# ScalarE applies the heads' norms in the launch block, and the low weight parts are dealt two and two to VectorE and GpSimd

## The chip, the cores and the metric

The kernel runs on one core of a Trainium2 chip. The metric is the time of one execution on the device in microseconds, lower is better. A core has TensorE (matrix products and turns into PSUM), VectorE, ScalarE and GpSimd (element by element work; the profile calls them PE, DVE, ACT and POOL), and SyncE, which issues DMAs here. Each engine works through its own queue in the order written; between engines, and where an engine reads what it has just written, semaphores order the work.

## The reference

The model has two layers, each of a cross attention, a self attention and a feed-forward part, on 256 tokens of width 512. All that this case touches are the projections at the head of the first one:

```python
def _ln(x, w, b):
    mu = jnp.mean(x, axis=-1, keepdims=True)
    var = jnp.mean(jnp.square(x - mu), axis=-1, keepdims=True)
    return (x - mu) * jax.lax.rsqrt(var + EPS) * w + b

def _fp8_linear_pertensor(x, wq, w_scale, in_scale):
    xq = _div_clamp_fp8(x, in_scale)
    return jnp.einsum('bsi,oi->bso', xq * in_scale, wq) * w_scale
...
ln_out = _ln(hidden_states, ln_w, ln_b)
q = _fp8_linear_pertensor(ln_out, wq, wq_scale, q_in_scale).reshape(b, s, g, hpg, d)
q = _ln(q, qln_w, qln_b)
k = _fp8_linear_pertensor(ln_out, wk, wk_scale, k_in_scale).reshape(b, s, g, d)
k = _ln(k, kln_w, kln_b)
v = _fp8_linear_pertensor(ln_out, wv, wv_scale, v_in_scale).reshape(b, s, g, d)
core = _gqa(q, k, v).reshape(b, s, nh * d)
qx = _fp8_linear_pertensor(ln_out, wqx, wqx_scale, qx_in_scale).reshape(b, s, g, hpg, d)
qx = _ln(qx, qxln_w, qxln_b)
```

Each head (128 columns) of q, qx and k gets a norm of its own over its columns; v gets none.

## The kernel before

The launch block is `front_stage`, the first stage with products. It cuts the four projections into twelve blocks of four heads (512 columns): four of q, four of qx, two of k, two of v. Each block is two steps, one for each half of the 256 tokens: steps 0 to 19 are those with a norm, 20 to 23 those of v. In the profile the names of this stage begin with `front_`.

**Weights.** A block's weights arrive in `raw` (three buffers, SyncE) as four slabs of 128x512. They are multiplied by the input scale and split into a rounded high part and the rest, the low part, so that a product of two passes keeps the precision. ScalarE makes the four high slabs (`high`, L2763). The low slabs are dealt by `POOL_KC` and `DVE_KC`: in a block with a norm VectorE makes slab 0 (`low`, one scalar_tensor_tensor, L2823) and GpSimd slabs 1 to 3, each with two operations (scale L2695, subtract L2702); in the blocks of v VectorE makes three and GpSimd one. High and low lie in a ring of four (`split`). A load into `raw` waits until high and both low halves of the block three before are done.

**A step.** TensorE makes the product of the step in eight 128x512 passes (`project`, L2732) into one of four PSUM tiles `mmp`. VectorE takes each head's mean and variance (`measure`: four bn_stats L2839, four bn_aggr L2842), ScalarE the root (`root`, L2779), VectorE the reciprocal (L2847) and then the norm itself, (product - mean) x rstd, one tensor_scalar for each of four heads (`normalise`, L2851) into `norm`, two buffers. TensorE turns the four heads (`turn`, L2742), and ScalarE puts them away with weight and bias (`put`, L2784). VectorE runs measure(s) ahead of normalise(s-1); TensorE runs project(s+3) right behind turn(s). Step s of VectorE also holds low(3 + s/2) for even s up to 16, and steps 4 and 8 a `quantise` (L2830 and L105 to L108), which makes the left operand for the next projection. ScalarE makes high(4 + s//2) in odd steps up to 15. In the first 40 us VectorE normalises x twice, and makes low(0) to low(3) and two quantises between.

All orders are written out by hand in each engine's loop. `measure(s)` waits for the count `norm` of step s-2, since `mv` and `stats` have two buffers; `link` makes an engine wait for its own operation.

## Time and profile before

| what | value |
|---|---|
| median of 3 runs | 2563.33 us (2561.70 to 2565.37) |
| the profiled execution | 2560.87 us |
| its span | 2559.1 us |
| mean granted TensorE clock | 0.959 |
| busy over the span: TensorE, VectorE, ScalarE, GpSimd | 89%, 70%, 47%, 23% |
| launch block, start to its last operation | about 4.9 to 130.4 us |

The profile comes from one execution. A group is a set of like instructions with its count, busy time and mean; a timeline row gives a start, a duration from the first start to the last end of the instructions merged in it, and what ended an idle stretch ahead of it. A waits row names who waited for whom. Of the span 5% is the launch block, and the stages behind it are left alone by the change.

### The profile page before, as it was taken

Reading aid. Unit: us, or ns where it says so; the run is one execution under the profiler, and the core shown is the slowest. Engines: PE = TensorE matmul, PEld = TensorE weight load, DVE = VectorE, ACT = ScalarE, POOL = GpSimd, SP = SyncE. Lnnn points to the kernel's source line nnn. Section 1 sums busy time; section 2 is a strip of 40 time slices with the busy share of each in tenths; the row PEclk is TensorE's granted clock in tenths of the full one; section 3 lists DMA queues with packets and bytes.
Section 4 is the critical chain, followed back from the end, with each engine's and each line's share of the span. In section 5 each row is a group of like instructions: output and inputs, shape, how many; then the busy total and the mean of one; then the engine's idle time right before and its main releaser. Section 6 shows DMA issues by size and latency. Waiting matters only on the chain. (4 is left out here: it accounts for less than half of the span.)

```text
span 2559.1 us, 31520 instructions
## 1 busy us (share of the span) xinstructions
PE 2279.3 (89%) x11472; PEld 1554.3 (61%) x11472; DVE 1786.6 (70%) x3422; ACT 1193.7 (47%) x1924; POOL 587.4 (23%) x435
## 2 busy tenths in 40 slices
PE   3779999999999999896897989788888779899998
PEld 2556666666666666564674456555556337677876
DVE  7856887777777778876896976666767754554444
ACT  4443466666566666633332114576766853211111
POOL 7810033334233333440000003323141300000000
PEclk9889999999999999998997999999999989899999
DMA  3331100000000100003544100000000013656661
GB/s 132 116 140 46 46 25 29 9 29 9 29 25 13 29 13 17 0 1 132 193 169 188 52 21 10 1 10 1 6 5 1 21 75 144 216 206 220 230 237 66
DMA packets 47622, 186.40 MB, mean 73 GB/s; under 512 B 6064, under 2 KB 10928, under 8 KB 37232
## 3 DMA queue, kind: packets, MB, share of 16 engines
q1 hardware_dynamic: 47472, 184.43, 20.0%
q8 instruction: 91, 1.49, 0.2%
q14 instruction: 59, 0.48, 0.1%
HBM read 174.71 MB, written 9.70 MB: 72 GB/s over the span
## 5 line engine op out<-in xcount | busy, mean ns | idle before, releaser
L406 PE MATMUL wide_a<-wide_w,ctxT 128*128 128x256 f32 (+1 forms) x2048 | 437.8, 367 | 2.8 <-POOL wide_eps L375 2.8
L406 PEld LDWEIGHTS wide_a<-wide_w,ctxT 128*128 128x128 f32 x2048 | 368.5, 191 | 76.5 <-issue 35.7
L388 POOL TENSOR_TENSOR wide_sums<-wide_sums,wide_s 128x512 f32<-128x512 f32 x224 | 301.3, 1345 | 461.8 <-ACT wide_s L536 448.6
L431 PE MATMUL wide_scores<-wide_q,wide_keysT 128*128 128x512 f32 x512 | 238.4, 604 | 12.5 <-ACT wide_s L532 12.5
L441 PE MATMUL wide_o<-wide_s,wide_values 128*128 128x512 f32 x512 | 233.8, 600 | 3.5 <-ACT wide_s L536 3.5
L532 ACT COPY wide_s<-wide_scores 128x512 f32<-128x512 f32 x256 | 148.4, 585 | 175.7 <-PE wide_scores L431 173.9
L1812 DVE TENSOR_REDUCE int_peaks<-int_a 128x1 f32<-128x1024 f32 x128 | 156.1, 1222 | 91.3 <-PE int_a L1535 90.1
L1535 PE MATMUL int_a<-int_keys,int_qrows 96*128 96x512 bf16 x512 | 151.8, 394 | 55.9 <-DVE int_peaks L1812 27.9
L1687 ACT ACTIVATE int_prob<-int_a,int_shift,int_qscale 128x1024 uint8<-128x1024 f32 x128 | 155.4, 1216 | 50.6 <-PE int_a L1535 50.1
L431 PEld LDWEIGHTS wide_scores<-wide_q,wide_keysT 128*128 128x128 f32 x512 | 87.9, 189 | 148.8 <-ACT wide_s L532 87.8
L594 DVE TENSOR_TENSOR wide_top<-wide_top,wide_s 128x512 f32<-128x512 f32 x240 | 165.6, 690 | 16.1 <-ACT wide_s L532 10.4
L2268 PEld LDWEIGHTS moe_bank<-moe_xb,moe_gate_up 128*128 128x128 f32 (+1 forms) x1536 | 162.0, 183 | 8.3 <-issue 8.3
L2268 PE MATMUL moe_bank<-moe_xb,moe_gate_up 128*128 128x96 f32 (+1 forms) x1536 | 162.6, 266 | 4.3 <-issue 4.3
L441 PEld LDWEIGHTS wide_o<-wide_s,wide_values 128*128 128x128 f32 x512 | 96.7, 192 | 100.2 <-issue 93.9
L607 DVE TENSOR_TENSOR wide_s<-wide_s,wide_peak_rows 128x2048 f32<-128x2048 f32 x64 | 146.8, 2294 | 0.8
L570 DVE BATCH_NORM_STATS2 wide_stats<-wide_keys 128x6 f32<-128x128 f32 x256 | 60.6, 278 | 110.9 <-ACT wide_values L514 108.4
L1446 PE MATMUL int_vp<-int_wk,ctxT_again 128*128 128x128 f32 x1024 | 126.6, 279 | 5.2 <-PEq L79 2.2
L1446 PEld LDWEIGHTS int_vp<-int_wk,ctxT_again 128*128 128x128 f32 x1024 | 122.7, 194 | 12.3 <-issue 4.0
L512 ACT COPY wide_keys<-wide_a 128x256 f32<-128x256 f32 x128 | 46.6, 364 | 174.3 <-PE wide_a L406 174.2
L536 ACT ACTIVATE wide_s<-wide_s 128x2048 f32<-128x2048 f32 x64 | 122.4, 1912 | 5.5 <-DVE wide_s L607 4.8
L1535 PEld LDWEIGHTS int_a<-int_keys,int_qrows 96*128 96x128 bf16 x512 | 37.0, 99 | 118.8 <-DVE int_peaks L1812 49.7
L2469 DVE TENSOR_REDUCE moe_coef<-moe_misc 96x1 f32<-96x4 f32 x32 | 5.1, 158 | 137.3 <-PE moe_misc L2277 137.3
(425 smaller groups left out, 4285.7 us busy)
## 6 DMA issues: line engine op xcount, KB each, us to landing
moe_gate_up<-hbm_m_gu SPq DMA_DIRECT2D x34, 1408.0 KB, 6.2
moe_down<-hbm_m_down_a SPq DMA_DIRECT2D x34, 512.0 KB, 6.9
causal_wqkv<-hbm_wqkv SPq DMA_DIRECT2D x8, 1536.0 KB, 6.6
ctxT<-hbm_ctxT SPq DMA_DIRECT2D x4, 2048.0 KB, 15.1
oproj_raw<-hbm_wproj SPq DMA_DIRECT2D x8, 1024.0 KB, 5.0
ctxT_again<-hbm_ctxT SPq DMA_DIRECT2D x4, 2048.0 KB, 21.6
wide_unit<-hbm_ffn_units SPq DMA_DIRECT2D x27, 256.0 KB, 2.7
ffn_early<-wide_unit SPq DMA_DIRECT2D x27, 256.0 KB, 2.0
```

What stands on the lines that cost most here:

```text
L388: ins = pool.tensor_tensor(sums[0][:, :], before, part[:, j, :], ALU.add)
L406: mm = pe.matmul(a[h][:, j, cols], ctxT[:, kc, t * P:(t + 1) * P], w[g % 2][:, kc, cols], start=(kc == 0), stop=(kc == KC - 1))
L431: pe.matmul(sp_[j % 2][:, :], keysT[:, j, :], q[:, :], start=True, stop=True).then_inc(s_s, 1)
L441: mm = pe.matmul(o[g % 2][:, :], values[m % VR][:, j, :], s[m % SR][:, j, :], start=(c == 0 and j == 0), stop=(c == QPG - 1 and j == 3))
L532: act.copy(s[n % SR][:, j, :], sp_[j % 2][:, :]).then_inc(s_se, 1)
L594: link(dve.tensor_tensor(top[:, :], before, s[n % SR][:, j, :], ALU.max))
L607: dve.tensor_tensor(s[m % SR][:, :, :], s[m % SR][:, :, :], peak_rows[:, :].unsqueeze(1).to_broadcast([P, 4, COLS]), ALU.subtract).then_in ...
L1446: mm = pe.matmul(vp[:, t * P:(t + 1) * P], ctxT[:, kc, i * P:(i + 1) * P], wk[:, kc, :], start=(kc == 0), stop=(kc == KC - 1))
L1535: mm = pe.matmul(wide[n % 2][:, z * 512:(z + 1) * 512], qrows[0:3 * HD, h, t * P:(t + 1) * P], keys[0:3 * HD, h % HC, j * 512:(j + 1) * 51 ...
L1687: act.activation(prob[u % 4][:, p * 1024:(p + 1) * 1024], wide[n % 2][:, :], ACT.Exp, bias=shift[:, u % NU:u % NU + 1], scale=qscale[:, t, ...
L1812: dve.tensor_reduce(peaks[u % 2][:, p:p + 1], wide[n % 2][:, :], AX.X, ALU.max).then_inc(s_ad, 1)
L2268: mm = pe.matmul(dst[0:m, j, :], wgu[i][:, kc, z * EI + f0:z * EI + f0 + m], xb[q % 2][:, kc, e % BATCH, :], start=(kc == 0), stop=(kc == ...
```

## The change

1. The deal of low slabs in the ten blocks with a norm becomes two and two: VectorE 0 and 1, GpSimd 2 and 3. The blocks of v stay.
2. VectorE no longer writes the norm. It makes the reciprocal and `centre` = -mean x rstd, a 128x4 operation, and counts `rstd` (`scale_of`). ScalarE's new `normalise` computes Identity(rstd x product + centre), one activation for each of four heads.
3. ScalarE runs root(s), then normalise(s-1), then put(s-2), then a high part. measure(s) keeps its wait for the norm of step s-2, which now is ScalarE's.

```diff
--- before.py
+++ after.py
@@ -2609,8 +2609,8 @@
                                               (3, "wv", 2, None, v)) for i in range(n)]
         NBK = len(blocks)
         NLN = 2 * sum(b[2] is not None for b in blocks)
-        POOL_KC = [range(1, KC) if b[2] is not None else range(3, KC) for b in blocks]
-        DVE_KC = [range(0, 1) if b[2] is not None else range(0, 3) for b in blocks]
+        POOL_KC = [range(2, KC) if b[2] is not None else range(3, KC) for b in blocks]
+        DVE_KC = [range(0, 2) if b[2] is not None else range(0, 3) for b in blocks]
         raw = [st.sb(f"raw{i}", [P, KC, HC * D]) for i in range(NRAW)]
         ring = [st.sb(f"split{i}", [P, 2, KC, HC * D], F32R) for i in range(NSPLIT)]
         scaled = [st.sb(f"scaled{i}", [P, HC * D]) for i in range(2)]
@@ -2631,15 +2631,16 @@
         mv = [st.sb(f"mv{i}", [P, HC, 2]) for i in range(2)]
         std = [st.sb(f"std{i}", [P, HC]) for i in range(2)]
         rstd = [st.sb(f"rstd{i}", [P, HC]) for i in range(2)]
+        centre = [st.sb(f"centre{i}", [P, HC]) for i in range(2)]
         norm = [st.sb(f"norm{i}", [P, HC, D]) for i in range(2)]
         mmp = [st.ps(f"mmp{i}", [P, HC, D]) for i in range(NMM)]
         tp = [st.ps(f"tp{i}", [P, HC, D]) for i in range(4)]
         s_x, s_scale, s_vec = st.sem("x_loaded"), st.sem("in_scales_loaded"), st.sem("vectors_loaded")
         s_raw = [st.sem(f"raw_loaded{i}") for i in range(NRAW)]
         names = ("identity var0 std0 norm0 turned0 lnT inverse divided quantised high low_dve low_pool eps "
-                 "products var std norm turned put stored dve pool")
+                 "products var std rstd norm turned put stored dve pool")
         (s_id, s_var0, s_std0, s_norm0, s_tp0, s_lnT, s_inv, s_y, s_q, s_hi, s_lod, s_lop, s_eps,
-         s_mm, s_var, s_std, s_norm, s_tp, s_put, s_st, s_dve, s_pool) = (st.sem(n) for n in names.split())
+         s_mm, s_var, s_std, s_rstd, s_norm, s_tp, s_put, s_st, s_dve, s_pool) = (st.sem(n) for n in names.split())
 
         def split(b):
             return ring[b % NSPLIT][:, 0, :, :], ring[b % NSPLIT][:, 1, :, :]
@@ -2775,8 +2776,17 @@
                     k = blocks[s // 2][0]
                     act.wait_ge(s_var, s + 1)
                     if s >= 2:
-                        act.wait_ge(s_norm, s - 1)
+                        act.wait_ge(s_rstd, s - 1)
                     act.activation(std[s % 2][:, :], mv[s % 2][:, :, 1], ACT.Sqrt, bias=eps_of[:, k:k + 1]).then_inc(s_std, 1)
+
+                def normalise(s):
+                    act.wait_ge(s_rstd, s + 1)
+                    if s >= 2:
+                        act.wait_ge(s_tp, s - 1)
+                    for h in range(HC):
+                        ins = act.activation(norm[s % 2][:, h, :], mmp[s % NMM][:, h, :], ACT.Identity, bias=centre[s % 2][:, h:h + 1],
+                                             scale=rstd[s % 2][:, h:h + 1])
+                    ins.then_inc(s_norm, 1)
 
                 def put(s):
                     _, _, ln, dst, i = blocks[s // 2]
@@ -2799,10 +2809,13 @@
                 act.wait_ge(s_eps, 1)
                 for s in range(NLN):
                     root(s)
+                    if s >= 1:
+                        normalise(s - 1)
                     if s >= 2:
                         put(s - 2)
                     if s % 2 and NSPLIT + s // 2 < NBK:
                         high(NSPLIT + s // 2)
+                normalise(NLN - 1)
                 for s in range(NLN, 2 * NBK):
                     k, _, _, dst, i = blocks[s // 2]
                     if s - 2 < NLN:
@@ -2842,15 +2855,13 @@
                         ins = dve.bn_aggr(mv[s % 2][:, h, :], stats[s % 2][:, h, :])
                     ins.then_inc(s_var, 1)
 
-                def normalise(s):
+                def scale_of(s):
                     dve.wait_ge(s_std, s + 1)
+                    if s >= 2:
+                        dve.wait_ge(s_norm, s - 1)
                     link(dve.reciprocal(rstd[s % 2][:, :], std[s % 2][:, :]))
-                    if s >= 2:
-                        dve.wait_ge(s_tp, s - 1)
-                    for h in range(HC):
-                        ins = dve.tensor_scalar(norm[s % 2][:, h, :], mmp[s % NMM][:, h, :], mv[s % 2][:, h, 0:1],
-                                                rstd[s % 2][:, h:h + 1], ALU.subtract, ALU.mult)
-                    ins.then_inc(s_norm, 1)
+                    dve.scalar_tensor_tensor(out=centre[s % 2][:, :], in0=mv[s % 2][:, :, 0], scalar=-1.0, in1=rstd[s % 2][:, :],
+                                             op0=ALU.mult, op1=ALU.mult).then_inc(s_rstd, 1)
 
                 dve.wait_ge(s_x, 16)
                 for r in range(2):
@@ -2887,12 +2898,12 @@
                 measure(0)
                 for s in range(1, NLN):
                     measure(s)
-                    normalise(s - 1)
+                    scale_of(s - 1)
                     if s in (4, 8):
                         quantise(s // 4 + 1)
                     if s % 2 == 0 and 3 + s // 2 < NBK:
                         low(3 + s // 2)
-                normalise(NLN - 1)
+                scale_of(NLN - 1)
                 dve.reciprocal(inv_smooth[:, :], smooth[:, :])
                 dve.tensor_tensor(wscale[:, :], scales[:, 4:5], scales[:, 5:6], ALU.mult)
```

VectorE's queue in the program of before, step 2 and the start of step 3 (`front_norm` is the count of norms done, `front_turned` that of turns):

```order
L2839 BN_STATS front_stats<-front_mmp 128x6 [waits front_norm,front_products]
L2839 BN_STATS front_stats<-front_mmp 128x6 x3
L2842 BN_AGGR front_mv<-front_stats 128x2 [waits front_dve]
L2842 BN_AGGR front_mv<-front_stats 128x2 x3
L2847 RECIPROCAL front_rstd<-front_std 128x4 [waits front_std]
L2851 TENSOR_SCALAR front_norm<-front_mmp,front_mv,front_rstd 128x128 [waits front_dve]
L2851 TENSOR_SCALAR front_norm<-front_mmp,front_mv,front_rstd 128x128 x3
L2823 SCALAR_TENSOR_TENSOR front_split<-front_raw,in_scales,front_split 128x512 [waits front_high]
L2839 BN_STATS front_stats<-front_mmp 128x6 [waits front_norm,front_products]
```

The same place of the changed program:

```order
L2852 BN_STATS front_stats<-front_mmp 128x6 [waits front_norm,front_products]
L2852 BN_STATS front_stats<-front_mmp 128x6 x3
L2855 BN_AGGR front_mv<-front_stats 128x2 [waits front_dve]
L2855 BN_AGGR front_mv<-front_stats 128x2 x3
L2862 RECIPROCAL front_rstd<-front_std 128x4 [waits front_std]
L2863 SCALAR_TENSOR_TENSOR front_centre<-front_mv,front_rstd 128x4 [waits front_dve]
L2836 SCALAR_TENSOR_TENSOR front_split<-front_raw,in_scales,front_split 128x512 [waits front_high]
L2836 SCALAR_TENSOR_TENSOR front_split<-front_raw,in_scales,front_split 128x512
L2852 BN_STATS front_stats<-front_mmp 128x6 [waits front_norm,front_products]
```

The four norms are gone from between a reciprocal and the next bn_stats, and the bn_stats still waits for `front_norm`, now a count of ScalarE's; the low operations are two.

ScalarE's queue before, steps 2 and 3 (`front_std` is the root, `qT` what put writes, `front_split` with 128x512 a high part):

```order
L2779 ACTIVATE front_std<-front_mv,front_eps_of 128x4 [waits front_norm,front_var]
L2784 ACTIVATE qT<-front_tp,head_vecs 128x4x128 [waits front_turned]
L2779 ACTIVATE front_std<-front_mv,front_eps_of 128x4 [waits front_norm,front_var]
L2784 ACTIVATE qT<-front_tp,head_vecs 128x4x128 [waits front_turned]
L2763 ACTIVATE front_split<-front_raw,in_scales 128x512 [waits front_products,front_raw_loaded2]
L2763 ACTIVATE front_split<-front_raw,in_scales 128x512 x3
```

And of the changed program:

```order
L2780 ACTIVATE front_std<-front_mv,front_eps_of 128x4 [waits front_rstd,front_var]
L2787 ACTIVATE front_norm<-front_mmp,front_centre,front_rstd 128x128 [waits front_rstd]
L2787 ACTIVATE front_norm<-front_mmp,front_centre,front_rstd 128x128 x3
L2794 ACTIVATE qT<-front_tp,head_vecs 128x4x128 [waits front_turned]
L2780 ACTIVATE front_std<-front_mv,front_eps_of 128x4 [waits front_rstd,front_var]
L2787 ACTIVATE front_norm<-front_mmp,front_centre,front_rstd 128x128 [waits front_turned,front_rstd]
L2787 ACTIVATE front_norm<-front_mmp,front_centre,front_rstd 128x128 x3
L2794 ACTIVATE qT<-front_tp,head_vecs 128x4x128 [waits front_turned]
L2764 ACTIVATE front_split<-front_raw,in_scales 128x512 [waits front_products,front_raw_loaded2]
```

Four activations on `front_norm` came in between root and put, waiting for `front_rstd`; the high part stands behind them and ahead of the next root.

## Rows read from the trace of the kernel before

**Rows 1.** Busy time by stretch: start:end, length, then engines, granted clock, DMA.
```profile
core 0: us, PE busy (x) PEld busy (x) DVE busy (x) ACT busy (x) POOL busy (x), PEclk, DMA share, GB/s
16.00:40.00 24.00, 9.73 (x32) 7.49 (x32) 21.04 (x25) 14.18 (x30) 23.22 (x14) 1.00 0.32 109
40.00:125.00 85.00, 56.27 (x227) 43.09 (x228) 78.52 (x285) 37.99 (x72) 74.70 (x50) 0.80 0.32 112
```

**Rows 2.** Groups up to 125 us: count, busy us, mean ns, idle before.
```profile
L2695 POOL TENSOR_SCALAR front_scaled<-front_raw,in_scales 128x512 f32<-128x512 f32 x32 | 57.4, 1793 | 7.8 <-DMA front_raw<-hbm_wq 7.8
...
L2702 POOL TENSOR_TENSOR front_split<-front_scaled,front_split 128x512 fp32r<-128x512 f32 x32 | 42.8, 1337 | 3.6 <-ACT front_split L2763 1.0
...
L2851 DVE TENSOR_SCALAR front_norm<-front_mmp,front_mv,front_rstd 128x128 f32<-128x128 f32 x80 | 27.3, 404 | 0.7
...
L108 DVE TENSOR_TENSOR front_quantised<-front_shifted,front_power 128x1024 fp32r<-128x1024 f32 x4 | 8.2, 2046 | 0.1
```

**Rows 3.** Waits up to 125 us: total us, times, longest.
```profile
ACT front_std L2779 <- DVE front_mv L2842: 51.0, 12, 9.1
...
PE front_tp L2742 <- DVE front_norm L2851: 29.2, 11, 8.0
```

**Rows 4.** Timeline of VectorE, step 5 and into 7: start, duration, operation, idle.
```profile
61.94 0.88 DVE L2839 BATCH_NORM_STATS2 front_stats<-front_mmp 128x6 f32<-128x128 f32 x4
...
63.15 0.14 DVE L2847 RECIPROCAL front_rstd<-front_std 128x4 f32<-128x4 f32 x1
63.33 1.37 DVE L2851 TENSOR_SCALAR front_norm<-front_mmp,front_mv,front_rstd 128x128 f32<-128x128 f32 x4
64.80 0.89 DVE L2839 BATCH_NORM_STATS2 front_stats<-front_mmp 128x6 f32<-128x128 f32 x4
...
69.32 0.89 DVE L2839 BATCH_NORM_STATS2 front_stats<-front_mmp 128x6 f32<-128x128 f32 x4 [1.09 <-PE front_mmp L2732]
```

**Rows 5.** Timeline of ScalarE in the same stretch.
```profile
63.47 0.76 ACT L2784 ACTIVATE qT<-front_tp,head_vecs 128x512 f32<-128x512 f32 x1
64.14 2.55 ACT L2763 ACTIVATE front_split<-front_raw,in_scales 128x512 fp32r<-128x512 f32 x4
66.58 0.29 ACT L2779 ACTIVATE front_std<-front_mv,front_eps_of 128x4 f32<-128x4 f32 x1
```

**Rows 6.** Groups of ScalarE over the whole span, shapes apart.
```profile
L2763 ACT ACTIVATE front_split<-front_raw,in_scales 128x512 fp32r<-128x512 f32 x48 | 30.6, 710 | 1.8 <-DMA front_raw<-hbm_wq 1.8
...
L946 ACT ACTIVATE causal_masked<-causal_masked,causal_inv 128x128 f32<-128x128 f32 x16 | 6.3, 393 | 7.2 <-DVE causal_inv L996 7.2
L2784 ACT ACTIVATE qT<-front_tp,head_vecs 128x512 f32<-128x512 f32 x8 | 6.1, 762 | 0.0
...
L2811 ACT ACTIVATE v<-front_mmp,scales 128x512 f32<-128x512 f32 x4 | 2.7, 683 | 1.6 <-PE front_mmp L2732 1.6
```

**Rows 7.** The line of VectorE's low slabs: count, shortest/median/longest ns, starts.
```profile
L2823 DVE SCALAR_TENSOR_TENSOR front_split<-front_raw,in_scales,front_split x16: 736/950/1783, 16.2 to 112.2; 128x512 fp32r<-128x512 f32 x16
```

**Rows 8.** Timeline of VectorE: first quantise, first bn_stats of a product, last quantise.
```profile
25.02 0.43 DVE L2830 TENSOR_SCALAR front_y<-front_y 128x1024 bf16<-128x1024 bf16 x1 [0.47 <-ACT front_y L2771]
...
29.31 2.20 DVE L108 TENSOR_TENSOR front_quantised<-front_shifted,front_power 128x1024 fp32r<-128x1024 f32 x1
...
39.99 0.88 DVE L2839 BATCH_NORM_STATS2 front_stats<-front_mmp 128x6 f32<-128x128 f32 x4
...
79.53 1.59 DVE L108 TENSOR_TENSOR front_quantised<-front_shifted,front_power 128x1024 fp32r<-128x1024 f32 x1
```

**Rows 9.** Timeline of TensorE: a turn, eight products, eight products later.
```profile
64.76 1.12 PE L2742 MATMUL front_tp<-ident,front_norm 128*128 128x128 f32 x4 [7.96 <-DVE front_norm L2851]
...
65.52 3.76 PE L2732 MATMUL front_mmp<-front_split,front_quantised 128*128 128x512 f32 x8
...
72.56 2.09 PE L2732 MATMUL front_mmp<-front_split,front_quantised 128*128 128x512 f32 x8
```

**Rows 10.** Timeline at the end of the stage.
```profile
129.74 0.69 ACT L2811 ACTIVATE v<-front_mmp,scales 128x512 f32<-128x512 f32 x1 [1.12 <-PE front_mmp L2732]
131.27 0.33 SPq L3079 DMA_DIRECT2D wide_w<-hbm_wkvx  x1
```

## The prediction

> **What bounds the kernel now.** The change lies in the launch block, the first stage, whose products end near 130 us of a span of 2559. I read it in this order. First the busy time by stretch [rows 1]: from 40 to 125 us, the loop over the twenty normalised steps, VectorE is busy 78.52 of 85.00 us and GpSimd 74.70, ScalarE only 37.99 and TensorE 56.27, at a granted clock of 0.80, between its two levels. From 16 to 40 us, ahead of the first measured product, VectorE is busy 21.04 of 24. Then the groups [rows 2]: the two GpSimd halves of a low part take 57.4 and 42.8 us, VectorE's norms 27.3. The waits say who ends them [rows 3]: ScalarE's root waits 51.0 us in all for VectorE's means and variances, and TensorE's turn waits 29.2 us for VectorE's norm. So in this stage VectorE is the chain, and TensorE and ScalarE follow it. GpSimd is nearly as full, but nobody is seen waiting for it. The last product's scaled copy is at 129.74 and the next stage's first load is issued at 131.27, so I let a microsecond won or lost here reach the end whole [rows 10].
>
> The step is best read in the timeline of VectorE [rows 4]. "Step s" starts with its bn_stats. From 61.94 to 64.80 is one step with nothing extra, 2.86 us: 1.21 for the four bn_stats and four aggregates, up to the reciprocal, 0.18 to the norm, 1.37 for the four norms, and 0.10 until the next bn_stats. From 64.80 to 69.32, 4.52 us, is a step with one low operation and a wait of 1.09 us for TensorE. ScalarE's row of work at the same place is put at 63.47, the four high parts from 64.14 for 2.55 us, the next root at 66.58 [rows 5]: 0.67 us for a put and 2.44 for a high, as spacings.
>
> **The change part by part.**
>
> (a) A new, serial link. The norm goes to ScalarE, and the bn_stats of step s+1 waits for the norm of step s-1 (the count front_norm), which ScalarE can only start once VectorE has made the scale and the centre of s-1 within step s. On VectorE it was its own work, now it is a round trip, and VectorE stands in it with nothing queued but the lows of every second step. The trace has no 128x128 Identity with a pointer for both scale and bias. By the rows [rows 6]: one of 128x128 with a pointer scale takes 393 ns from SBUF; put, with two pointers, takes 762 where the copy of v, with one, takes 683, so the second pointer is 79; the same two sizes from SBUF and PSUM, 710 and 683, take off 27. That is 445 ns for one; four high parts take 2.55 us at 710 each, so neighbours stand 0.61 apart, 0.10 less than one lasts. Four norms: 3 x 0.345 + 0.445 = 1.48 us, 1.38 of ScalarE's time. Bounds: 1.25 us (plain 393 less 27 and spaced by 0.29) to 1.7 (four of 0.43 spacing). The centre, a scalar_tensor_tensor of 128x4, is an operation of the reciprocal's size, 0.14 to 0.2 us; I take 0.16. A plain step is then 1.21 to the reciprocal, 0.18, 0.16, 0.04 to ScalarE, 1.48, 0.04 back: 3.11 against 2.86. Nine plain steps at +0.25: **+2.3 us**.
>
> The Trainium skill (ScalarE: Activation LUTs, "What ACT_TABLE_LOAD costs") gives 186 ns plus 0.833 per element, 93 for each pointer operand and 93 of overlap; by it the four norms take 1.64 us, and the plain steps would cost 1.4 us more than in my sum. Its "Rules for kernel authors" also puts multiply and add on VectorE, not ScalarE, which speaks against this change.
>
> (b) The same link on the steps that ScalarE shares with a high part. Let the norm of an even step end at T. ScalarE then has a put (0.67) and the high part (2.44) queued ahead of the next root, so the high part of the block lands at T+3.1; VectorE's lows of the same block come in the next step, at T+1.6, and wait for it. Two lows then end at T+3.1 + 1.9 = T+5.0, and the next bn_stats is at T+5.1. The ScalarE branch (root 0.2, norm 1.48) ends at T+4.8, just ahead. So such a step lasts 5.05 us. Before it lasted 4.52 where TensorE's products ran slowly behind a quantise [rows 4, 9] (steps 6 and 10; step 2 likewise, but without a put ahead, so it stays), and 2.67 + 0.74 = 3.4 where they did not (step 12): 2 x 0.5 + 1.65 = **+2.7 us**. The blocks of v keep three lows, but these start at 3.07 into the step, not 2.67: **+0.8 us** for both.
>
> (c) The second low operation outside these steps. One takes 736 ns at least and 950 in the median, up to 1783, of 16 [rows 7]. I take 0.95. In the four blocks ahead of the loop VectorE has one idle stretch to hide it, 0.47 us before the first quantise [rows 8]: 4 x 0.95 - 0.47 = **+3.3 us** (2.5 with 0.74, 5.0 with 1.37). In the two steps that hold a quantise, the four norms (1.37) leave, the centre (0.16) and a low (0.95) come: 2 x -0.26 = **-0.5 us**.
>
> (d) The end. The last two norms stood behind one another on VectorE (1.28 + 0.18 + 1.37); now they are ScalarE's, with a put between them (0.16 + 0.04 + 1.38 + 0.67 + 1.48): **+0.9 us**.
>
> (e) What GpSimd gives up. Ten pairs of its operations leave, 10 x (1.79 + 1.34) = 31 us of 100 [rows 2]. Nobody is seen waiting for it, so this by itself is worth nothing (below that, nothing either: its loads are let go earlier, not later, though each still waits for VectorE's low too). What it gives is less collision on VectorE. The same work takes 736 or 1783 ns in a low [rows 7]; L108 takes 1.59 us at 79.53 and 2.05 in the mean [rows 2, 8], which is 0.22 of it. If the whole of a quantise (25.02 to 31.51, 6.5 us [rows 8]) is stretched like this, that is 1.45 us in each of four, 5.8 in all. With 31 of 100 us of GpSimd gone I take a third: **-1.9 us**, between 0 and -5.8.
>
> A sentence of the Trainium skill agrees in kind: GPSIMD Engine Reference, "Key points", says that GpSimd shares its SBUF interfaces with VectorE, in contention with VectorE's instructions with two SBUF inputs. A low is such a one, so the half that VectorE takes over is of the kind that collides, at the moment when both wait for the same high part.
>
> Sum: 2.3 + 2.7 + 0.8 + 3.3 - 0.5 + 0.9 - 1.9 = +7.6 us. The profiled execution took 2560.87 us (span 2559.1), 2.5 below the median of the three runs, 2563.33; the difference carries over: 2571.0.
>
> **The rivals.**
>
> Rival 1, the busy time decides: VectorE sheds 27.3 us of norms, takes 20 x 0.16 and ten lows (9.5), -14.6 us, 2549. For it speaks that VectorE is the fullest engine and ScalarE half idle. Against it: bn_stats waits for front_norm in the very next place of VectorE's queue, and nothing else is queued there in every second step. It would need the norm to be hidden behind something. Chance 0.07.
>
> Rival 2, the relief of GpSimd is worth more: lows near 0.74 everywhere and quantises near their shortest. Then (c) is 2.5 - 0.9, (b) loses 1.3 and the relief is 4 to 6 instead of 1.9: +1 to +2, 2565. For it: GpSimd now has pauses. Against: in the early stretch it stays busy (23.22 of 24 us now), and both engines start on the same high part. Chance 0.28.
>
> Rival 3, slower still, TensorE's clock: after a pause the clock is granted at the lower level, and eight products take 3.76 us and a turn 1.12, against 2.09 at the higher one [rows 9]; from the turn's start at 64.76 to the end of the products are 4.5 us. In the loop after the change the norm of an odd step ends at T+4.8; a turn and eight products at the lower level come to T+9.3, where VectorE's own chain has the second next bn_stats at T+8.2. It decides once the pause of about 2 us per block is enough to keep the clock down; each such block costs 1.1 us, five of them 5.5: +13, 2576. Against it: a longer chain of TensorE keeps TensorE busier, and so tends to end itself. Chance 0.15.
>
> That the change does not do what it says is out: all four ScalarE norms stand in the order in each of the 20 steps, and each block has two lows on either engine.
>
> **How the numbers follow.** Forecast 0.50, 2571.0, itself from +3.5 to +11 by the bounds of the norm and the lows. Rivals 0.07, 0.28, 0.15. Leaving out rival 1 (0.07) and about half a tenth at either edge, the range is 2560 to 2578. A measurement of this kernel can tell some 0.2%, 5.1 us, from no change. Slower by more than that: 0.40 of the forecast's 0.50 and rival 3, 0.55. Within: the forecast's lower end and nearly all of rival 2, 0.36. Faster: 0.09.
>
> **What would show it.** In the profile of the changed kernel: bn_stats of a plain step 3.1 us apart, with an idle stretch of VectorE of about 1.5 us before it, released by ScalarE's norm; norms spaced 0.35 us; steps 6, 10 and 12 near 5 us, ended by the lows behind the high part; first bn_stats of a product near 43 us instead of 39.99 [rows 8]; GpSimd waiting for the high parts; the last copy of v near 137 us instead of 129.74. It is wrong if a norm on ScalarE takes under 0.3 us in spacing, if the lows run at 0.74, or if the first bn_stats comes before 42.

## The result: slower by 0.17%

The changed kernel takes 2565.28 us in the median of 20 runs (2560.17 to 2567.64), the kernel before 2561.89. The ratio is 1.0017 with a 95% interval of 1.0009 to 1.0025: 4 us slower, between 2 and 6. The ratio leaves out one run of the kernel before that took 9195 us. A second series, run later beside fresh runs of the kernel before, gave 1.003 (1.0019 to 1.0041), so 5 to 10 us. The forecast was +7.7 us. The place and the links were as forecast. Several terms were badly sized, and they nearly cancelled.

The busy time by stretch, as in [rows 1] (start:end, length, the engines, granted clock, DMA), of the changed kernel:

```profile
16.00:40.00 24.00, 9.07 (x32) 7.06 (x32) 22.82 (x26) 13.73 (x28) 23.50 (x14) 1.00 0.44 150
40.00:125.00 85.00, 51.57 (x201) 38.00 (x202) 59.42 (x219) 59.93 (x137) 49.96 (x30) 0.81 0.28 97
```

VectorE, 78.52 of 85 before, is busy 59.42; ScalarE went from 37.99 to 59.93, GpSimd from 74.70 to 49.96. No engine is near full any more, and still the stage is longer. That is how a chain through several engines looks. The groups up to 140 us, which answer to [rows 2] (count, busy us, mean ns, idle before):

```profile
L2696 POOL TENSOR_SCALAR front_scaled<-front_raw,in_scales 128x512 f32<-128x512 f32 x22 | 41.8, 1899 | 9.1 <-DMA front_raw<-hbm_wq 7.4 <-DMA front_raw<-hbm_wv 1.7
...
L2703 POOL TENSOR_TENSOR front_split<-front_scaled,front_split 128x512 fp32r<-128x512 f32 x22 | 33.9, 1540 | 28.4 <-ACT front_split L2764 27.3
...
L2787 ACT ACTIVATE front_norm<-front_mmp,front_centre,front_rstd 128x128 f32<-128x128 f32 x80 | 30.2, 464 | 0.6 <-DVE front_centre L2863 0.6
L2836 DVE SCALAR_TENSOR_TENSOR front_split<-front_raw,in_scales,front_split 128x512 fp32r<-128x512 f32 x26 | 27.6, 1103 | 9.3 <-ACT front_split L2764 8.7 <-DVE front_quantised L108 0.3
L2852 DVE BATCH_NORM_STATS2 front_stats<-front_mmp 128x6 f32<-128x128 f32 x80 | 17.7, 281 | 17.1 <-ACT front_norm L2787 14.9 <-PE front_mmp L2733 2.2
```

The norms, 27.3 us on VectorE, are 30.2 on ScalarE. The columns behind the bar are new: VectorE's bn_stats sat idle 14.9 us for ScalarE's norm, its lows 8.7 us for ScalarE's high part, and GpSimd 27.3 us for the same high part. Before, VectorE waited for neither in the loop. The waits up to 140 us, as in [rows 3]:

```profile
PE front_tp L2743 <- ACT front_norm L2787: 35.0, 17, 8.6
ACT front_std L2780 <- DVE front_mv L2855: 30.5, 12, 9.4
...
DVE front_stats L2852 <- ACT front_norm L2787: 14.9, 9, 1.7
```

ScalarE's wait for VectorE (51.0) has shrunk to 30.5, and its counterpart has appeared.

One block of two steps in VectorE's timeline, steps 5 and 6, as in [rows 4]:

```profile
64.96 0.49 DVE L2863 SCALAR_TENSOR_TENSOR front_centre<-front_mv,front_rstd 128x4 f32<-128x4 f32 x1
67.10 0.89 DVE L2852 BATCH_NORM_STATS2 front_stats<-front_mmp 128x6 f32<-128x128 f32 x4 [1.64 <-ACT front_norm L2787]
...
70.14 2.44 DVE L2836 SCALAR_TENSOR_TENSOR front_split<-front_raw,in_scales,front_split 128x512 fp32r<-128x512 f32 x2 [1.48 <-ACT front_split L2764]
72.49 0.88 DVE L2852 BATCH_NORM_STATS2 front_stats<-front_mmp 128x6 f32<-128x128 f32 x4
```

and ScalarE's and GpSimd's beside it, as in [rows 5]:

```profile
65.49 1.50 ACT L2787 ACTIVATE front_norm<-front_mmp,front_centre,front_rstd 128x128 f32<-128x128 f32 x4 [0.29 <-DVE front_centre L2863]
66.88 0.79 ACT L2794 ACTIVATE qT<-front_tp,head_vecs 128x512 f32<-128x512 f32 x1
67.54 2.56 ACT L2764 ACTIVATE front_split<-front_raw,in_scales 128x512 fp32r<-128x512 f32 x4
...
70.25 1.77 POOL L2703 TENSOR_TENSOR front_split<-front_scaled,front_split 128x512 fp32r<-128x512 f32 x1 [3.93 <-ACT front_split L2764]
```

The bn_stats of step 6 (67.10) starts when the norm of step 4 has ended (65.49 + 1.50). VectorE is ready for its lows at 68.66, but the high part of that block ends at 70.10. VectorE and GpSimd then start on it together, and the two lows take 2.44 us. At the end of the stage, as in [rows 10], the last copy of v:

```profile
136.53 0.69 ACT L2824 ACTIVATE v<-front_mmp,scales 128x512 f32<-128x512 f32 x1 [1.12 <-PE front_mmp L2733]
```

It was at 129.74, so the stage lost 6.79 us. The span is 5.2 us longer (2564.3 against 2559.1).

### The profile page after: what moved, and what is told of

Its sections match the earlier page's. It is cut to its first block and busy times, and to the rows that moved or that the text cites. A ratio compares the mean times of both kernels' runs of the same rounds, so it can differ in the third digit from the quotient of the medians.

```text
span 2564.3 us, 31548 instructions
## 1 busy us (share of the span) xinstructions
PE 2278.3 (89%) x11472; PEld 1555.5 (61%) x11472; DVE 1771.8 (69%) x3372; ACT 1223.0 (48%) x2004; POOL 563.9 (22%) x415
## 5 line engine op out<-in xcount | busy, mean ns | idle before, releaser
L406 PE MATMUL wide_a<-wide_w,ctxT 128*128 128x256 f32 (+1 forms) x2048 | 437.3, 367 | 2.8 <-POOL wide_eps L375 2.8
L406 PEld LDWEIGHTS wide_a<-wide_w,ctxT 128*128 128x128 f32 x2048 | 368.4, 191 | 76.6 <-issue 36.0
L1535 PE MATMUL int_a<-int_keys,int_qrows 96*128 96x512 bf16 x512 | 150.6, 391 | 57.2 <-DVE int_peaks L1812 30.5
L1694 ACT CAST int_probT<-int_b 128x1024 bf16<-128x1024 uint8 x88 | 89.2, 1014 | 23.0 <-PE int_b L1547 22.9
```

The source lines that it names most:

```text
L406: mm = pe.matmul(a[h][:, j, cols], ctxT[:, kc, t * P:(t + 1) * P], w[g % 2][:, kc, cols], start=(kc == 0), stop=(kc == KC - 1))
L1535: mm = pe.matmul(wide[n % 2][:, z * 512:(z + 1) * 512], qrows[0:3 * HD, h, t * P:(t + 1) * P], keys[0:3 * HD, h % HC, j * 512:(j + 1) * 51 ...
```

## The experiments

I read each of them first by the start of the last copy of v, which ends the stage, and then by its series against the kernel before. Steps are named as in the prediction. A ratio stands with its 95% interval.

**A yardstick.** The kernel before and the changed kernel, each run again unchanged, with a trace and a series.

> The kernel before, unchanged, as a yardstick: a second trace and a second series. Every theory expects a ratio of 1.000 with an interval that holds it; last copy of v within 0.5 us of 129.74. If the trace or the series differs by more, differences of that size between kernels say nothing.

> The changed kernel, unchanged: a second trace and series beside the kernel before on the same chip. Theory: last copy of v within 0.5 us of 136.53, ratio 1.001 to 1.003. If the last copy is the same and the ratio goes below 1.001, part of the stage's loss is given back behind it.

| | last copy of v | span | ratio to the kernel before |
|---|---|---|---|
| kernel before, again | 129.58 (129.74) | 2558.6 | 0.9996 (0.9981 to 1.0011) |
| changed kernel, again | 136.43 (136.53) | 2562.9 | 1.003 (1.0019 to 1.0041) |

The last copy of v agrees within 0.2 us between the two traces of a kernel. Inside the stage the two traces of the changed kernel stand up to 0.5 us apart: its first bn_stats of a product is at 43.30 and 43.76. Behind the stage they wander by 2 to 3 us: the first wide product group (L406) of the kernel before was 2.3 us later in its second trace and that of the changed kernel 3.0 us earlier (200.2 instead of 203.2). So the last copy of v is the sharp measure. The spans differ by 5.2 and 4.3 us, less than the stage's 6.8, and the wander is too large to say whether the later stages give part of the loss back.

**One part at a time.**

```diff
-        POOL_KC = [range(2, KC) if b[2] is not None else range(3, KC) for b in blocks]
-        DVE_KC = [range(0, 2) if b[2] is not None else range(0, 3) for b in blocks]
+        POOL_KC = [range(1, KC) if b[2] is not None else range(3, KC) for b in blocks]
+        DVE_KC = [range(0, 1) if b[2] is not None else range(0, 3) for b in blocks]
```

> The norm goes to ScalarE as in the changed kernel, but the low slabs stay dealt one to VectorE and three to GpSimd. Theory A (the round trip to ScalarE costs, the new deal costs at the start and pays back in the two steps with a quantise): first bn_stats of a product near 40.0 us, as before; plain steps 3.2 us; a quantise stays near 6.2 us or more since GpSimd has no pauses; steps 6, 10 and 12 fall to about 4.7 us, ended by ScalarE's norm instead of the lows; last copy of v near 135 us, 4 to 6 us after the kernel before, the median about +3 to +5. Rival B (the deal is what costs, the norm's move is hidden): last copy of v at or ahead of 130 us, median 0 or less.

The other way round, the kernel before with only the deal of the changed one (the same two lines, the other way):

> VectorE keeps the norm; the low slabs are dealt two and two. Theory A: first bn_stats of a product near 43.3 us; plain steps 2.86 us; the steps with a quantise shorter by about 1 us (the quantise itself near 5 us, a second low of 0.8); step 12 longer by 1.2 us; last copy of v about 132 us, +2; median +1 to +3. Rival B: the last copy near 135 us or later, most of the loss of the changed kernel.

| | first bn_stats of a product | quantises in the loop | last copy of v | ratio |
|---|---|---|---|---|
| before | 39.99 | 6.76, 6.23 | 129.74 | |
| norm alone | 39.72 | 6.50, 5.97 | 134.66 (+4.9) | 1.002 (1.0008 to 1.0033) |
| deal alone | 43.71 | 6.43, 6.43 | 133.51 (+3.8) | 1.0019 (1.0007 to 1.0031) |
| both | 43.30 | 4.81, 4.81 | 136.53 (+6.8) | 1.0017 (1.0009 to 1.0025) |

Each part is a loss by itself; the series don't order the three kernels, the last copies do. Norm alone came out as theory A said but for its plain steps, which took 3.2 to 3.7 us instead of 3.2. Deal alone cost nearly twice the forecast (3.8 us instead of 2): I had the quantises shrink, since GpSimd has fewer slabs, and they did not, 6.43 us each against 6.76 and 6.23. The first and the last operation of the 6.76 us, in the kernel before:

```profile
54.16 0.60 DVE L2830 TENSOR_SCALAR front_y<-front_y 128x1024 bf16<-128x1024 bf16 x1
...
58.73 2.19 DVE L108 TENSOR_TENSOR front_quantised<-front_shifted,front_power 128x1024 fp32r<-128x1024 f32 x1
```

GpSimd's operations of fewer slabs stand at the same place, beside the quantise. GpSimd's timeline there, in the kernel with the deal alone:

```profile
57.17 1.27 POOL L2702 TENSOR_TENSOR front_split<-front_scaled,front_split 128x512 fp32r<-128x512 f32 x1 [2.23 <-ACT front_split L2763]
58.43 1.73 POOL L2695 TENSOR_SCALAR front_scaled<-front_raw,in_scales 128x512 f32<-128x512 f32 x1
60.24 1.31 POOL L2702 TENSOR_TENSOR front_split<-front_scaled,front_split 128x512 fp32r<-128x512 f32 x1
61.54 2.53 POOL L2695 TENSOR_SCALAR front_scaled<-front_raw,in_scales 128x512 f32<-128x512 f32 x1
```

against a quantise from 57.83 to 64.26. In the changed kernel GpSimd's first operation on the block comes later, since the high part is late:

```profile
58.76 2.05 POOL L2703 TENSOR_TENSOR front_split<-front_scaled,front_split 128x512 fp32r<-128x512 f32 x1 [1.94 <-ACT front_split L2764]
```

The quantise starts at 57.08 there, and of its five operations only the last is stretched (2.17 us; 1.26 with GpSimd idle, below):

```profile
57.08 0.42 DVE L2843 TENSOR_SCALAR front_y<-front_y 128x1024 bf16<-128x1024 bf16 x1
57.54 0.43 DVE L105 TENSOR_SCALAR front_power<-front_y 128x1024 uint16<-128x1024 uint16 x1
58.00 0.43 DVE L106 TENSOR_SCALAR front_power<-front_power 128x1024 bf16<-128x1024 bf16 x1
58.46 1.23 DVE L107 TENSOR_TENSOR front_shifted<-front_y,front_power 128x1024 f32<-128x1024 bf16 x1
59.72 2.17 DVE L108 TENSOR_TENSOR front_quantised<-front_shifted,front_power 128x1024 fp32r<-128x1024 f32 x1
```

That is why both together (+6.8) cost less than the sum (+8.7): the late high part keeps GpSimd out of the quantise's way. Steps 4 and 8 bear it out. By the starts of the bn_stats they changed together by -1.6 us with the norm alone, +0.2 with the deal alone and -5.1 with both.

**What GpSimd's company costs.** From block 4 on, GpSimd works on 8 of the 512 columns of a slab in both kernels, so most of its low slabs are left out.

```diff
-                    return pool.tensor_scalar(scaled[n % 2][:, :], raw[b % NRAW][:, kc, :], in_scales[:, k, kc:kc + 1], None, ALU.mult)
+                    w = HC * D if b < 4 else 8
+                    return pool.tensor_scalar(scaled[n % 2][:, :w], raw[b % NRAW][:, kc, :w], in_scales[:, k, kc:kc + 1], None, ALU.mult)
...
-                    ins = pool.tensor_tensor(lo[:, kc, :], scaled[n % 2][:, :], hi[:, kc, :].bitcast(F32), ALU.subtract)
+                    w = HC * D if b < 4 else 8
+                    ins = pool.tensor_tensor(lo[:, kc, :w], scaled[n % 2][:, :w], hi[:, kc, :w].bitcast(F32), ALU.subtract)
```

> The kernel before, but from block 4 on GpSimd works on 8 of a slab's 512 columns, so most of its low slabs are left out and GpSimd is idle from about 54 us. The time is read for VectorE's operations alone. Theory E (GpSimd's operations stretch VectorE's): the two quantises in the loop fall from 6.76 and 6.23 us to 4.1 to 4.3, a low is 0.74 throughout, plain steps stay 2.86; last copy of v 5 to 7 us earlier, about 124 us. Rival F (the quantise is shorter in the changed kernel for another reason, ScalarE's or TensorE's traffic): the quantises stay at 6.2 or more.

> The changed kernel with the same: from block 4 on GpSimd works on 8 columns of a slab. Theory E: quantises from 4.81 to about 4.2 us, a pair of lows behind a high part from 2.43 to 1.5, so the steps 6, 10 and 12 fall from 5.39 to about 4.8 and are then ended by ScalarE's norm; last copy of v 5 to 6 us earlier, 131 us. Rival F: both stay.

Each ran once (2550.42 and 2559.00 us, beside a median of 2558.38 of the kernel before), so they are read by their traces. Both quantises in the loop fell to 3.90 us in either kernel, from 6.76 and 6.23 before and 4.81 after. From 58 us on a low takes 0.74 to 0.75 in the kernel before and a pair 1.42 to 1.44 in the changed one, where it took 2.44 behind a high part. The last operation of the quantise, in the changed kernel with GpSimd idle, to be set beside the 2.17 us above:

```profile
59.31 1.26 DVE L108 TENSOR_TENSOR front_quantised<-front_shifted,front_power 128x1024 fp32r<-128x1024 f32 x1
```

The last copy of v is at 120.40, 9.3 us earlier than before, and at 128.68, 7.9 us earlier than in the changed kernel. Theory E holds, and by more than I had put down. It also gives the price of the rest: with GpSimd out of the way the change costs 8.3 us, more than with it. What GpSimd's company costs stands most plainly in the centre's line (count, shortest/median/longest ns). First the changed kernel with GpSimd idle, then the changed kernel, then the one with the lows moved (below):

```profile
L2865 DVE SCALAR_TENSOR_TENSOR front_centre<-front_mv,front_rstd x20: 161/161/165, 45.7 to 120.8; 128x4 f32<-128x4 f32 x20
```

```profile
L2863 DVE SCALAR_TENSOR_TENSOR front_centre<-front_mv,front_rstd x20: 161/162/492, 45.9 to 128.6; 128x4 f32<-128x4 f32 x20
```

```profile
L2863 DVE SCALAR_TENSOR_TENSOR front_centre<-front_mv,front_rstd x20: 161/164/1278, 45.9 to 125.7; 128x4 f32<-128x4 f32 x20
```

Four columns, 0.16 us, can take 1.28 us. In the kernel with the lows moved VectorE's and GpSimd's timelines show what it waits for:

```profile
63.95 1.19 DVE L2863 SCALAR_TENSOR_TENSOR front_centre<-front_mv,front_rstd 128x4 f32<-128x4 f32 x1
63.86 1.27 POOL L2703 TENSOR_TENSOR front_split<-front_scaled,front_split 128x512 fp32r<-128x512 f32 x1
```

The centre started just behind a subtraction and ended with it (65.14 and 65.13).

**The links.** First the wait for the norm. When bn_stats of step s+1 runs, nobody still reads its buffers: the root and the centre of step s-1 are done, and ScalarE's norm reads the scale and the centre, not the mean.

```diff
                 def measure(s):
                     dve.wait_ge(s_mm, s + 1)
                     if s >= 2:
-                        dve.wait_ge(s_norm, s - 1)
+                        dve.wait_ge(s_rstd, s - 1)
```

> The changed kernel, but the bn_stats of step s+1 waits for VectorE's own scale and centre of step s-1 instead of for ScalarE's norm of it: its buffers are free by then. Theory A (the round trip is what makes a block 8.6 us long): VectorE's 1.65 us of idle time per plain step goes, the next limit is ScalarE's own work, about 7.0 us for a block with a high part; last copy of v near 128 us (124 to 131), median 5 to 9 us below the changed kernel, at or below the kernel before. Rival C (ScalarE or TensorE is the limit already, and the wait only shows it): the last copy stays at 135 us or later, and another wait takes the 14.9 us.

The same with four buffers for scale and centre (`rstd[s % 4]`, `centre[s % 4]`, and the scale's wait three steps back):

> As own_count, and with four buffers for the scale and the centre, so that VectorE may run ahead of ScalarE's norms by more steps. Theory A: if ScalarE is the limit after own_count, this gives less than 1 us more. Rival C: as for own_count. If the two buffers still bind, it is 2 us or more ahead of own_count.

The last copy came at 135.68 and 136.46, only 0.9 and 0.1 us earlier, and the two kernels differ by no more than their starts do (first bn_stats at 43.24 and 43.52); ratios to the kernel before 1.0012 (1.0002 to 1.0022) and 1.0014 (1.0004 to 1.0023). Theory A as I had written it fell: the round trip alone was not what made the block long. What came is what rival C had put down, a last copy at 135 us or later and another wait in the place of the first; whether ScalarE's or TensorE's own work is the limit, as that rival said, is settled by the next runs. VectorE's waits from 40 to 125 us with its own count:

```profile
DVE front_split L2836 <- ACT front_split L2764: 14.4, 6, 3.0
DVE front_stats L2852 <- PE front_mmp L2733: 5.2, 6, 1.8
```

The 14.9 us for the norm are gone. The lows' wait for the high part took most of their place, 14.4 instead of 8.2 in that stretch, and the lows start at the same point of the block as before, 6.6 us after the bn_stats of step 5 (69.74 - 63.17, and 70.14 - 63.58): the high part stands behind the norm in ScalarE's queue, the lows behind the high part, the next bn_stats behind the lows. Starting early only lets VectorE wait longer there. Another 5.2 us went to waits for TensorE's products, of which the changed kernel has none in this stretch.

So I formed theory D, a chain of norm, put, high part, two colliding lows and bn_stats, and moved the lows one step later, where the high part has landed:

```diff
-                    if s % 2 == 0 and 3 + s // 2 < NBK:
+                    if s % 2 and s >= 3 and 3 + s // 2 < NBK:
                         low(3 + s // 2)
```

> The changed kernel with each of VectorE's lows in the loop moved one step later, into the step where VectorE waits 1.65 us for ScalarE's norm anyway; the wait for the norm stays. Theory D (formed on own_count: the chain of a block is high part, then VectorE's two lows, then the next bn_stats, and the round trip is only the second limit behind it): the steps that held the lows fall from 5.4 to about 4.8 us, the plain ones stay near 3.2 since the lows hide in them, the steps with a quantise lose their low, 1.6 us: last copy of v near 131 us (129.5 to 133), median 3 to 6 us below the changed kernel. Theory A (the round trip alone): under 2 us.

> Both: bn_stats waits for VectorE's own count, and the lows stand one step later. Theory D: with neither link left, a block falls from 8.6 us to ScalarE's own work, 7.0 us (two roots, two times four norms, two puts, one high part); last copy of v 124 to 127 us, 3 to 6 us below the kernel before. Rival C (TensorE at its lower clock is the limit): blocks near 8.5 to 9, last copy at 132 or later.

| | wait of bn_stats | lows | last copy of v | ratio |
|---|---|---|---|---|
| changed | norm | even steps | 136.53 | 1.0017 (1.0009 to 1.0025) |
| own count | own | even steps | 135.68 | 1.0012 (1.0002 to 1.0022) |
| lows later | norm | odd steps | 133.60 | 1.001 (0.9998 to 1.0021) |
| both | own | odd steps | 126.89 | 0.9983 (0.9973 to 0.9993) |

One link removed brings 0.9 or 2.9 us, both together 9.6. So neither ScalarE's nor TensorE's own work was what held the changed kernel. The move alone fell short of its forecast (131): the steps that had held the lows did fall, from 5.39 to 4.69, but the plain ones rose from 3.20 to 4.2 or 4.3, since the centre, now beside GpSimd's subtractions, took up to 1.28 us, and the two lows (1.77 us) stand behind it. A block of the two was 9.0 us long, no shorter than the 8.6 before; the 2.9 us come from the two steps with a quantise, 6.5 us instead of 7.98 without their lows, and from the blocks with three lows. With both links removed such a block took 7.8 to 8.8 us, not the 7.0 that I had expected: VectorE then waits 15.4 us for TensorE's products.

**The start.** The deal's second low ahead of the loop, taken back for the first four blocks:

```diff
-        POOL_KC = [range(2, KC) if b[2] is not None else range(3, KC) for b in blocks]
-        DVE_KC = [range(0, 2) if b[2] is not None else range(0, 3) for b in blocks]
+        POOL_KC = [range(1, KC) if n < 4 else range(2, KC) if b[2] is not None else range(3, KC) for n, b in enumerate(blocks)]
+        DVE_KC = [range(0, 1) if n < 4 else range(0, 2) if b[2] is not None else range(0, 3) for n, b in enumerate(blocks)]
```

> As own_lows_later, with the first four blocks dealt one and three as before, the others two and two. Theory D: the first bn_stats of a product is back near 40.0 us, 3.3 earlier, and all of it reaches the end: last copy of v 121 to 124 us. Against: GpSimd has three pairs in each of the first four blocks again, and its part of block 3 was done only 0.9 us before its product in the kernel before; if that binds, the gain is under 2 us and TensorE waits for front_low_pool.

> VectorE keeps the norm and its own order; the first four blocks are dealt one and three as before, blocks 4 to 9 two and two. It is own_later_deal without the norm's move. Theory D: the first bn_stats is back at 40.0 us, the loop is that of deal_alone (84 us from the first bn_stats to the last, against 80.3 before and 73.6 in own_later_deal), so the last copy of v is near 129.7 us and the median within 0.1% of the kernel before: the gain of own_later_deal then comes from the norm on ScalarE, once no link holds it. Rival G (the gain of own_later_deal is the deal's): last copy near 123 us, median 0.3% lower.

With both links gone and this deal, the first bn_stats is at 39.78 and the last copy at 123.23. It takes 2551.15 us in the median, ratio 0.9967 (0.9954 to 0.9979), 5 to 12 us less than the kernel before: it beats both kernels. The same deal with the norm left on VectorE ends at 130.13, ratio 1.0003 (0.9993 to 1.0013), so rival G falls. The deal by itself is worth nothing; the norm on ScalarE is what pays, once nothing waits for it in turn. In the best version VectorE waits for another engine. Its two largest waits from 40 to 125 us:

```profile
DVE front_stats L2852 <- PE front_mmp L2733: 15.7, 9, 4.0
DVE front_stats L2852 <- DVE front_quantised L108: 0.4, 2, 0.2
```

and TensorE's products behind a quantise, timeline:

```profile
63.01 1.11 PE L2743 MATMUL front_tp<-ident,front_norm 128*128 128x128 f32 x4 [3.94 <-ACT front_norm L2787]
...
63.77 3.76 PE L2733 MATMUL front_mmp<-front_split,front_quantised 128*128 128x512 f32 x8
...
71.71 2.09 PE L2733 MATMUL front_mmp<-front_split,front_quantised 128*128 128x512 f32 x8
```

After a pause of 3.94 us eight products take 3.76 us instead of 2.09, as in [rows 9]; the granted clock is 0.50 from 63 to 67.5 us and 1.00 from 71.8 to 73.8. TensorE's turns in turn wait 26.4 us in this stretch for ScalarE's norms, so the chain still runs through several engines, and no run here shows what would shorten it further.

## Why the prediction was right, and where its steps failed

It said slower, by +7.6 us in the stage; the stage lost 6.8. The series say +4 (2 to 6) and +8 (5 to 10). By its steps, from the starts of the bn_stats in the two traces:

| term | forecast | measured |
|---|---|---|
| (c), (e) second lows and two quantises ahead of the loop | +3.3, and half of -1.9 | +3.3 (39.99 to 43.30) |
| (a) nine plain steps | +2.3 | +3.7 |
| (b) steps 2, 6, 10, 12, with a high part | +2.7 | +4.0 |
| (b) steps 14 and 16, three lows | +0.8 | +0.2 |
| (c), (e) steps 4 and 8, with a quantise | -0.5, and half of -1.9 | -5.1 |
| step 18 | 0 | +0.3 |
| (d) the end | +0.9 | +0.3 |
| sum | +7.6 | +6.8 |

From the second traces the terms come out within 0.1 of these, but for the first (+3.8) and step 18 (-0.1).

**The sum is nearer than its terms, and that is luck.** The start, the plain steps, the steps with a high part and step 18 were 3.9 us too cheap together; steps 4 and 8, the three lows and the end were 4.8 too dear. The time says even less: 2565.28 us is the number that rival 2 had (2565) rather than the forecast's 2571.0, and only the stage's +6.8 tells the two apart. By the prediction's own mark of 5.1 us the first series, +4, is no change, to which it gave 0.36, and the second, +8, is slower.

**The norm on ScalarE was sized right.** Forecast 445 ns and 1.48 us for four; measured 464 in the mean and 1.51. The Trainium skill's formula (ScalarE: Activation LUTs, "What ACT_TABLE_LOAD costs") gave 1.64 for four and 479 ns for one: for four the trace is nearer to the estimate from the rows, and its single norm lies between the two. The plain step was forecast at 3.11 and came at 3.17 to 3.28. Steps 5 and 9 took 3.52, their centre 0.49 instead of 0.16 beside GpSimd; I had taken the centre's price from an undisturbed operation.

**The link behind the high part was right, the lows in it too cheap.** I had the step at 5.05, it was 5.39: the pair takes 2.44 us, not 1.9. The prediction had even said that both engines start on the same high part, and still used the median of all lows, from places where they do not meet. The operations to price it by were among those of [rows 7], above the median.

**The relief of GpSimd was mis-sized most.** For steps 4 and 8 the prediction had -0.5 and about -1.0, and they gave back 5.1. The two quantises in them lost 3.4 us. The two ahead of the loop, for which the term had another -1.0, grew by 0.4 together (6.49 and 6.44 before, 6.21 and 7.09 after). The size was taken from L108 alone, 1.45 us of stretch in a quantise; with GpSimd idle a quantise takes 3.90, so up to 2.9 of 6.76 were stretch. And the term assumed that a third less GpSimd work means a third less stretching. The deal alone shows that this rule is wrong: with a third less work the quantises stayed at 6.43 us. What matters is whether GpSimd's operations lie beside the quantise. In the changed kernel they start 1.7 us into it, for a reason I had in hand (GpSimd would wait for the high parts, as the last part of the prediction says) and did not carry over to the quantise. The two steps gave back 2.5 and 2.6 us. Of this 1.95 and 1.42 are the quantise itself, the rest the norms that left less the second low.

**The start came out at (c)'s number for other reasons.** (c) counted 0.47 us of idle time in which second lows could hide. VectorE's timeline in the kernel before has a longer stretch, ahead of its copy of the turned columns:

```profile
21.35 1.90 DVE L2879 TENSOR_SCALAR front_lnT<-front_tp,ln 128x256 f32<-128x256 f32 x4 [1.46 <-PE front_tp L2716]
```

In the changed kernel 0.38 us of it are left. Against this the eight lows took 4.4 us more than the four, not 3.8, and the quantises there grew.

**The end** came cheaper than forecast: behind the last norms TensorE had products of v to do either way, so a part of what (d) added lay beside work. The turn of the last norm, at 132.24 us, follows eight of them (130.31, 2.09 us) without a wait.

**The rivals.** Rival 1, that VectorE's busy time decides, was wrong for this kernel, for the reason given: nothing else was queued behind the wait. It is what the best version reaches for: its last copy of v is 6.5 us ahead of the kernel before, where rival 1 had 14.6. Rival 2, a larger relief, was right in its mechanism for the quantises in the loop and wrong for the lows, and it explains why the loss stayed below the forecast. Rival 3, TensorE's clock, hardly showed in the changed kernel: the granted clock of 40 to 125 us was 0.81 against 0.80. The pauses of about 2 us a block that this rival had feared were there, and mostly the products behind them took 2.1 us still. TensorE's timeline:

```profile
60.25 0.66 PE L2743 MATMUL front_tp<-ident,front_norm 128*128 128x128 f32 x4 [2.18 <-ACT front_norm L2787]
60.66 2.10 PE L2733 MATMUL front_mmp<-front_split,front_quantised 128*128 128x512 f32 x8
```

It is the same at 80.33 and 100.42. At 109.41 and 123.30 eight products took 3.21 and 3.40 us (granted clock 0.60 and 0.57). Only step 19 waited for a product, the latter, 2.24 us; in the second trace step 19 came without such a delay. In the version with both links removed TensorE is the one waited for.

What the prediction and my first expectations missed as reasoning: (b) had both branches, ending at T+5.1 and T+4.8, but as terms of a sum, and I then treated the wait for the norm as the main defect and expected 128 us from removing it alone. The experiments say that there were two links of nearly the same length side by side, the norm's round trip and the high part with its lows, and that either alone was enough to hold the block at 8.6 to 9.0 us.

## What to carry to other kernels

Moving work off the fullest engine pays only if that engine has something else to do meanwhile: after the move, look at what it has queued next and at which wait stands there, and drop waits that were free only because the engine waited for itself. When two chains of like length run side by side, removing either shows little (0.9 and 2.9 us here) and removing both shows far more than the sum (9.6). Two engines that disturb one another are to be kept apart in time; giving one of them less work at the same place left the disturbed operations as long as they were (two quantises of 6.43 us, 6.76 and 6.23 before).

## What the runs showed of the hardware

- GpSimd's company stretches VectorE's operations by up to about the length of one of GpSimd's: a scalar_tensor_tensor of 128x4 took 161 to 165 ns with GpSimd idle and up to 1278 ns beside subtractions of 1.27 us; a chain of five operations on 128x1024 took 3.90 us alone and 6.2 to 7.1 beside it. It goes both ways: GpSimd's subtraction took from 1.26 up to 2.06 us, its scaling from 1.55 up to 2.53. The Trainium skill (GPSIMD Engine Reference, "Key points") names this contention for two SBUF inputs and for two-port modes; the traces agree for two inputs, and add the size. Which mode an operation ran in they don't show; the quantise's bf16 tensor_scalar (L106) took 0.43 us with GpSimd idle and up to 1.39 beside it.
- In the changed kernel ScalarE's Identity of 128x128 from PSUM with scale and bias from pointers took 447 to 493 ns, and four followed one another in 1.50 to 1.52 us.
- Two traces of a kernel stood up to 0.5 us apart inside the stage, within 0.2 us at its end and up to 3 us apart at the start of the next products, so a change of a few microseconds in an early stage is read better from the stage's end than from the span.
